# A state-space mixer and a ternary MLP on one core: weight parts and weight copies at other times of a block, and another order in the last step

## The reference, cut to what matters

```python
# layer 1: x + mixer(layernorm(x))
proj = xn @ W_in * mup_vector                      # 512 -> 1024 z, 1280 xBC, 64 dt
xBC = silu(causal_conv(xBC, conv_w, 4 taps) + conv_b)
dt = softplus(dt + dt_bias); dA = exp(dt * -exp(A_log))
state = state * dA_t + (dt_t * x_t) B_t;  y_t = state . C_t      # scan over tokens
g = (y + D * x) * silu(z)
g = g * rsqrt(mean(g * g) + 1e-5) * norm_w
x1 = x + g @ W_out
# layer 2: x1 + mlp(layernorm(x1)), weights of -1, 0 and 1, scales per row
hdn = silu((x1n @ gate_w.T) * gate_s) * ((x1n @ up_w.T) * up_s)
out = x1 + (hdn @ down_w.T) * down_s
```

## Time and profile before

| | us |
|---|---|
| median of 3 runs | 797.53 |
| lowest and highest | 793.96, 797.57 |
| the profiled execution, its own time | 789.45 |
| span of its trace | 787.6 |

### The profile page before, as it was taken

How to read it: one execution, slowest core, us unless ns; L and a number is a source line. 1 busy time by engine, 2 the same in 40 slices (tenths; PEclk the granted TensorE clock), 3 DMA queues, 4 the chain that set the end, 5 groups by cost and what they waited for, 6 DMA issues and landing times.

```text
span 787.6 us, 20256 instructions
## 1 busy us (share of the span) xinstructions
PE 745.6 (95%) x8464; PEld 612.6 (78%) x8464; DVE 521.9 (66%) x843; ACT 493.8 (63%) x941; POOL 292.4 (37%) x232
## 2 busy tenths in 40 slices
PE   5878999999999999999999999689999999999997
PEld 4856878888788888888787887477878878887885
DVE  6878978987977987977988886735423532632331
ACT  6989888877978978978878978623312321321330
POOL 2164186285375465455546636410010011001002
PEclk9988999999999999999999999789999999999999
DMA  9832337637548448348446454685013013003002
GB/s 300 228 85 84 77 93 213 141 87 235 109 96 245 118 95 247 92 100 216 130 115 170 136 117 120 204 276 179 0 55 108 0 42 119 0 13 94 1 1 82
DMA packets 41929, 94.94 MB, mean 121 GB/s; under 512 B 9648, under 2 KB 15280, under 8 KB 41648
## 3 DMA queue, kind: packets, MB, share of 16 engines
q1 hardware_dynamic: 41840, 93.67, 42.6%
HBM read 84.73 MB, written 17.57 MB: 130 GB/s over the span
## 4 chain that ended last, share of the span: by engine, by line
PE 51%; DVE 26%; ACT 8%; DMA 8%; issue 5%; SPq 1%; POOL 0%; DVEq 0%; POOLq 0%; ACTq 0%
DVE cx L874 10%; PE ps_x L1549 10%; PE ps_y L1562 10%; PE ps_proj L1549 8%; PE ps_x L1198 3%; DVE ring L929 3%; PE ps_proj L1149 3%; DVE dt_p L849 3%; PE ps_y L1221 3%; PE ps_proj L1150 3%; PE ps_proj L1151 2%; ACT ring L658 2%; DVE state L939 2%; PE ps_x L1232 2%; ACT sz L601 2%
## 5 line engine op out<-in xcount | busy, mean ns | idle before, releaser
L487 POOL TENSOR_TENSOR ring<-tokd,ring 128x1024 f32<-128x1024 f32 x64 | 123.2, 1937 | 197.0 <-ACT tokd L653 125.8
L1149 PE MATMUL ps_proj<-xn_hi,win_hi 128*128 128x256 f32 x608 | 178.9, 294 | 1.5 <-DVE xn_lo L843 1.5
L1150 PE MATMUL ps_proj<-xn_lo,win_hi 128*128 128x256 f32 x608 | 172.6, 284 | 0.0
L1151 PE MATMUL ps_proj<-xn_hi,win_lo 128*128 128x256 f32 x608 | 172.1, 283 | 0.0
L1149 PEld LDWEIGHTS ps_proj<-xn_hi,win_hi 128*128 128x128 f32 x608 | 116.4, 191 | 15.6 <-issue 11.4
L1150 PEld LDWEIGHTS ps_proj<-xn_lo,win_hi 128*128 128x128 f32 x608 | 116.6, 192 | 0.4
L1151 PEld LDWEIGHTS ps_proj<-xn_hi,win_lo 128*128 128x128 f32 x608 | 116.5, 192 | 0.0
L874 DVE SCALAR_TENSOR_TENSOR cx<-cin,consts,cx 128x256 f32<-128x256 f32 x240 | 96.4, 481 | 0.0
L1440 POOL TENSOR_TENSOR res<-res,hidden 128x512 f32<-128x512 f32 x16 | 20.5, 1283 | 184.0 <-DVE hidden L1503 184.0
L929 DVE TENSOR_TENSOR ring<-ring,ps_tok 128x1024 f32<-128x1024 f32 x64 | 75.6, 1214 | 4.2 <-ACT ring L662 4.2
L658 ACT ACTIVATE ring<-ring 128x1024 f32<-128x1024 f32 x64 | 66.8, 1059 | 10.6 <-POOL ring L487 10.6
(11 more groups left out here) (154 smaller groups left out, 1615.8 us busy)
## 6 DMA issues: line engine op xcount, KB each, us to landing
ring<-cum_dram SPq DMA_DIRECT2D x128, 256.0 KB, 5.4
xin<-x SPq DMA_DIRECT2D x8, 512.0 KB, 4.3
res<-x SPq DMA_DIRECT2D x32, 128.0 KB, 3.0
x_dram<-res SPq DMA_DIRECT2D x32, 128.0 KB, 2.4
x_in_sb<-x_dram SPq DMA_DIRECT2D x4, 1024.0 KB, 5.7
res<-x_dram SPq DMA_DIRECT2D x16, 256.0 KB, 2.7
out<-res SPq DMA_DIRECT2D x16, 256.0 KB, 2.0
gate_w_copy<-gate_w SPq DMA_DIRECT2D x2, 1408.0 KB, 9.1
```

The costliest lines, as they stand in the source:

```text
L487: pool.tensor_tensor(ring[:, g, :, :], own, ring[:, g, :, :], ALU.subtract).then_inc(diffed, 1)
L1149: pe.matmul(out, win_hi[:, k, cols], xn_hi[:, k, :], start=(k == 0), stop=False)
L1150: pe.matmul(out, win_hi[:, k, cols], xn_lo[:, k, :], start=False, stop=False)
L1151: made = pe.matmul(out, win_lo[:, k, cols], xn_hi[:, k, :], start=False, stop=(k == KT - 1))
```

## The change

**Parts.** The 18 parts get widths 1024, 1024 and 768 for each half of a weight, where there were five of 1024 and one of 512. There are still three in a block. Their tiles are now `xin`, `rows` and a tile of their own, `low_buf`. In block i, SP loads the first into `xin` and the third into `low_buf` where it loaded x and the third part before, and the second into `rows` at the end of its list. DVE reduces them a block later: two right after `gate_lo` of the block's start, the third after the first step's gate.

**x and copies.** The x of the next block is loaded at the start of a block, after the first reduction has freed `xin`. The copies are 12 pieces of 704 KB, two at the start of each of the blocks 2 to 7, ahead of the x1 store and the ring loads of step 1.

**Last step.** The gated y of step 15 is split into a part of h_hi and h_lo instead of g_hi and g_lo, and projected into ps_x instead of ps_out, so its split waits neither for `project_out(14)` nor its projection for `make_x1(14)`. The first half of `project_out(14)` stands between carry and add_carry. DVE makes x1 of step 13 before `mix(15, 0)`. The four normalisations of the MLP's input are parted around `gate_lo`, and `any_low` and `make_x1(14)` come later. SP loads x1 for the statistics before it waits for `all_low_max`.

```diff
-LOW_W = 1024
-LOW_EACH = -(-HID * INTER // (P * LOW_W))
+LOW_WIDTHS = (1024, 1024, 768)
+LOW_EACH = 2 * len(LOW_WIDTHS)
 LOW_PARTS = 3 * LOW_EACH
+LOOKED = range(1, 1 + LOW_PARTS // len(LOW_WIDTHS))
+COPIES = 12
...
+        def g_of(c):
+            if c < LAST:
+                return g_hi, g_lo
+            return [t[:, ZT:ZT + 2, :].rearrange("p m (k t) -> p (m k) t", t=P) for t in (hand.h_hi, hand.h_lo)]
+        def out_of(c):
+            return ps_out[:] if c < LAST else ps_x[:, 0:BT]
...
-                w, rows_of = n // 2, slice((n % 2) * (P // 2), (n % 2 + 1) * (P // 2))
+                w, rows_of = n // 4, slice((n % 4) * (P // 4), (n % 4 + 1) * (P // 4))
...
             def body(i, first, last):
-                looking = not first and not last
+                if i - 1 in LOOKED:
+                    if i + 1 < BLOCKS:
+                        sp.wait_ge(hand.low_max_made, 3 * (i - 2) + 1)
+                        load_x(i + 1)
+                    keep_weights(2 * (i - 2))
+                    keep_weights(2 * (i - 2) + 1)
                 if not first:
                     store_x1(i - 1, 0)
                     load_res(i, 0, first)
                 for g in range(GROUPS):
-                    if looking and g == 2:
-                        load_low_rows(3 * (i - 1), STEPS * i)
-                    if looking and g == GROUPS - 1:
-                        load_low_xin(3 * (i - 1) + 1, i)
                     load_cums(i, 1, g)
-                if looking:
-                    keep_weights(i - 1)
...
-                if i + 2 < BLOCKS:
-                    if looking:
-                        sp.wait_ge(hand.low_max_made, 3 * (i - 1) + 2)
+                if i in LOOKED:
+                    load_low_xin(i)
+                    load_low_buf(i)
+                else:
                     load_x(i + 2)
-                if looking:
-                    load_low_rows(3 * (i - 1) + 2, STEPS * i + 1)
...
                 load_whole(i + 1, False)
+                if i in LOOKED:
+                    load_low_rows(i)
...
             body(BLOCKS - 1, False, True)
-            sp.wait_ge(hand.low_all_made, 1)
-            sp.dma_start(hand.low_row[:], hand.low_all[:]).then_inc(hand.low_in, 16)
             sp.wait_ge(projected, EVENTS * BLOCKS)
             sp.dma_start(hand.xin[:], hand.x1_by_block[0]).then_inc(hand.x_in, 16)
...
             load_weights(1)
+            sp.wait_ge(hand.low_all_made, 1)
+            sp.dma_start(hand.low_row[:], hand.low_all[:]).then_inc(hand.low_in, 16)
...
             def gate_hi(c):
                 act.wait_ge(gate_made, c + 1)
-                act.wait_ge(out_made, c)
+                if c < LAST:
+                    act.wait_ge(out_made, c)
...
                 if tiles[0] == 0:
                     pe.wait_ge(g_split, c + 1)
-                    pe.wait_ge(x1_made, c)
+                    if c < LAST:
+                        pe.wait_ge(x1_made, c)
...
                 carry(i, 1)
+                if last:
+                    project_out(c - 1, FIRST_HALF)
...
                     sum_squares(c - 1)
-                    project_out(c - 1)
+                    project_out(c - 1, SECOND_HALF)
```

94 lines of the change are left out of this document (53 added, 41 removed).

## The result

The changed kernel takes 786.97 us, the median of 6 runs (783.21 to 789.96), and the kernel before 795.75 us (792.48 to 798.62, 6 runs) beside it. The ratio is 0.9889 with a 95% interval of 0.9848 to 0.9929: 8.8 us less, and the interval lies wholly under 1. The forecast was 790.4, the range 785.5 to 796.5. Of the 3.4 us between forecast and result about half is in the gain, 8.8 us for 7.1. The other half is in the kernel before, whose median of six is 795.75 where the forecast started from 797.53.

A forecast was written before the change was run, and what follows sets the result against it. PE bounds the kernel, busy for 745.6 of 787.6 us, so only its holes and slow clock can be won. 2.2 us in the blocks plus 4.9 in the last step make 7.1: 797.53 - 7.1 = 790.4 us, range 785.5 to 796.5.

The forecast's parts named there:

- The start of a block: DVE's extra part of 1.21 us at a block's start costs nothing; data up to 0.8 us later cost nothing either.
- the prediction's sign of being wrong: Wrong if PE still waits on DVE at mixer's end, weight loads begin after 506, or rows' part ends DVE idle time.
- slower* rival: At a block's start the part in rows lands late and DVE stalls before xpad: 801.8 us, chance 0.08.
- The middle of a block: Blocks' nine PE holes of 4.3 us shrink as the chain gains 0.3 to 0.4 us a block: 2.2 us, bounds 0 to 4.3.
- The copies: Copies at a block's start, in a window of free DMA, cost nothing, or up to 1 us a block if transfers are slower.
- The first hole: Last step, PE's wait of 2.36 us before carry: stays, and carry stays slow, ending at 500.05.
- The hole at rows: Last step, PE's 3.37 us wait for rows: gone or below 0.5 us, filled by the half projection; rows done at 502.6.
- PE ready for the MLP: Last step, end of PE's chain: ready at about 519.5, 9 us before 528.50.
- The weights: Late next: loads begin at some 503.3, all in at 521.7, MLP at 522.2, 523.6 in effect; gain 4.9 us.
- The second x load: The MLP's second x load comes behind the weights and moves with them.
- second rival: Queue gives it back: x1(13) store waits for 2.7 MB, loads begin at 506.6, 2.8 us gained, 794.7 us; chance 0.2.
- its second term: Last step, up to the MLP's first product: gain 528.5 - 523.6 = 4.9 us, bounds 9 and 2.

The follow-up runs named there:

- copies_mid_fixed: Changed kernel with the two weight copies of blocks 2 to 6 behind the ring loads, those of block 7 still at its start: 787.87 us, 0.9878 to the kernel before.
- blocks_only: Kernel before with the parts, the x load and the copies moved, last step as before: 793.59 us, ratio 0.9951.
- before_again: The kernel before, unchanged, run and profiled once more: 795.51 us.
- tail_only: Kernel before with the last step's edits alone: 792.69 us, ratio 0.9941.
- copies_back: Changed kernel with the two copies of each block behind the ring loads: 791.58 us, 0.9921 to the kernel before.
- after_again: The changed kernel once more, on the same chip as the runs of its two halves: 787.09 us, 0.9879 to the kernel before.
- no_xin_part: Kernel before without the weight part in xin: its load gone, its scan cut to two columns of rows: 792.41 us, ratio 0.9918.
- weights_first: Changed kernel with gate and up weights loaded ahead of the store of x1 of step 13 and the load of res: 788.76 us, 0.9899 to the kernel before.
- half_old: Changed kernel with the whole projection of step 14 behind the groups again: 787.81 us, 0.9877 to the kernel before.
- x1_old: Changed kernel with make_x1(13) behind the first mix, the statistics and the carry's scaling again: 788.86 us, 0.9902 to the kernel before.
- stores_early: Changed kernel with gate and up weights first, and the stores of steps 14 and 15 moved among the down weights: 784.76 us, 0.9827 to the kernel before.
- g_old: Changed kernel with step 15's gated y and projection in the other steps' buffers again, make_x1(14) ahead of the MLP's low halves: 786.08 us, 0.9839 to the kernel before.

## Why the prediction was right, point by point

**The start of a block** is free, as forecast. There is no wait for the part in `rows` but 0.3 us once (up to 1.1 us in the other profiles with these blocks, in copies_mid_fixed), and what DVE waits there for ACT's copy of tok shrank from 17.3 to 8.5 us in the stretch. Taken literally the prediction's sign of being wrong, that this part ends an idle time of DVE, did appear; but up to 0.8 us of it was reckoned as free. The *slower* rival had no part in it.

**The middle of a block** is the term of the sum that was mis-sized: 2.2 us forecast, 3.9 us measured by blocks_only, and 4.0 us by the profiles (369.4 us is the mean of three with the old blocks, before, before_again and tail_only, and 365.4 us that of ten with the new). The step taken, "hardly any of it counts, because gate_lo also waits for ACT's g_hi", is right for g_lo itself: in before g_lo begins 0.03 us after g_hi's end in five of the six blocks. What the sum left out stands behind g_lo. The three dt_p instructions took 1.05 to 2.66 us there for 0.93, 5.0 us too much over the six blocks, next to a last ring that came late behind the load of the part in `xin`. The prediction saw that the rings would come earlier without that load, but put it down as 0.35 us for ScalarE alone. It also read one block. Block 6, which it read, has no hole; block 5 has PE's largest one:

```profile
376.88 2.66 DVE L849 SCALAR_TENSOR_TENSOR dt_p<-dt_p,dt_e 128x128 f32<-128x128 f32 x3
```

```profile
380.93 1.94 PE L1198 MATMUL ps_x<-state,cx 128*64 128x512 f32 x8 [1.45 <-DVE xpad L915]
```

Its upper bound of 4.3 us was the sum of the holes in that execution; 6.6 and 7.0 stood in the next two. The two profiles that the prediction was about show no gain in the blocks at all, 366.34 and 366.38 us.

**The copies** cost nothing in the blocks, as forecast (copies_mid_fixed). That their place in block 7 sets when the weights may be read was not seen; copies_back put 3.3 to 4.5 us on it.

**The first hole** stayed, 2.36 us. The slow carry behind it, 3.38 us before, is 1.94 in the profile of after and 3.46 in after_again; see the last section.

**The hole at rows** was to be gone, or below 0.5 us, and is 1.06 us. The steps were nearly exact. All times in this and the next two points are less 2.70 us, by which after is late at carry 14. DVE has rows done at 502.7 (forecast 502.6). PE has the half projection done at 501.6 where 503.0 was forecast, since the carry ran at full clock; so the 1.06 us are the other side of what the clock saved. In after_again, where the carry took 3.46 us, there is no hole at rows.

**PE ready for the MLP**: 519.5 forecast, 520.7 measured. Two idle times put down to issue, 0.90 and 2.29 us, are in it, and the forecast had neither: its 0.9 us at the last group are for the products themselves. Before had such an idle time as well, 1.50 us inside the groups. What it is stays open.

**The weights** are what is late next, as forecast. Their loads began at 505.2, not at 503.3: the store took 5.55 us behind the 2.7 MB for 3.42 in before, and here the trace agrees with the order of a ring that the prediction drew from the Trainium skill, page "DMA: Bandwidth & Descriptors", section "Queues, rings and completion order". It was the second rival's mechanism, with 1.9 of its 3.3 us. All parts were in at 522.6 (forecast 521.7), since the loads themselves took 17.4 us in place of 18.4, and the MLP began at 523.5 where 522.2 was forecast. The 1.4 us for a slow clock behind that wait did not come (the first eight products take 2.1 us). The two errors cancel: 523.6 in effect against 523.5, and 4.97 us of the gain against 4.9 forecast. tail_only confirms the term by time, 4.7 us.

**The second x load** was said to move with the weights. In after it came 58.95 us after carry 14 (537.00 less 478.05), and in before 62.84 (538.19 less 475.35). So it moved 3.9 of the 5.0 us, and the rest shows as PE's wait of 1.29 us for 0.36. From the row of before:

```profile
538.19 0.39 SPq L1393 DMA_DIRECT2D x_in_sb<-x_dram  x1
```

**Not in the prediction at all**: the stretch up to carry 2, where the change edits no instruction that has run by then, took 111.67 us for 109.01. Over the profiles it is 110.9 us in the mean for the ten kernels with the changed blocks and 109.5 for the other four.

In stages, by means over the profiles, the gain is 4.0 us in the blocks and 5.1 us behind carry 14 (314.5 us in before, before_again, blocks_only and no_xin_part, 309.4 in after, after_again, tail_only and copies_mid_fixed), less 1.4 us at the start: 7.7 us. The forecast of 7.1 us was right for its second term. For the sum it was lucky: 1.8 us too little in the blocks and 1.4 us that it didn't have at the start offset each other. Its chances of faster, 0.57, 0.15 and 0.02, add up to 0.74, not 0.73; nothing hangs on it.

## What to carry to other kernels

One profile is one draw of the transfers' landing times. Where an engine's list waits for a transfer that is only just in time, look at the same wait in every block, not at one that happens to be covered. And follow the engine's list from there to where the bottleneck waits, with the length of every instruction beside its shortest: here the wait in plain sight came to less, in the sums, than three small instructions behind it that had grown from 0.93 to as much as 2.66 us. When a wait at the end of a stage is for transfers, list what stands behind them in the same queue before moving them ahead: the 3.2 us that weights_first won came back at the next thing in that queue.

## What the runs showed of the hardware

**The clock behind one and the same hole fell in some executions and not in others.** In all 14 profiles PE is idle for 2.36 or 2.37 us before the carry of step 15. The carry then takes 1.94 us in six (after, half_old, x1_old, copies_mid_fixed, stores_early, blocks_only) and 2.54 to 3.55 us in the other eight. Granted clock by windows (us; busy PE, PEld, DVE, ACT, POOL; clock, DMA share, GB/s), in after and in before_again:

```profile
496.00:500.00 4.00, 1.64 (x16) 1.10 (x14) 3.81 (x8) 3.97 (x5) 3.63 (x4) 1.00 0.90 291
```

```profile
500.00:504.00 4.00, 3.53 (x8) 0.68 (x8) 2.50 (x4) 4.00 (x5) 3.84 (x4) 0.58 1.04 417
```

The first stays at the level of 2.4 GHz, the second falls towards 1.2. The same kernel had both: 1.94 us in after, 3.46 in after_again. In eight profiles the half projection follows the carry at once, and the two together can be measured, from the carry's start to the end of the twelfth matmul. They take 4.88 to 4.91 us in three (after, copies_mid_fixed, stores_early) and 6.43 to 6.54 us in the other five, with nothing between. Even copies_back, where the carry took only 2.54 us, is one of the five: there the slow clock came later and reached into the half projection. So the price of this hole was nothing or some 1.6 us, and the 1.44 us that the prediction put on every hole of over 2 us is that second value, less what falls behind the carry. What decides between the two, no run here shows.

**VectorE sometimes takes over twice as long for the same instructions.** DVE in before and in after, at the same place in block 0:

```profile
60.16 1.40 DVE L821 SCALAR_TENSOR_TENSOR wout_lo<-skip,consts,wout_hi 128x512 fp32r<-128x512 f32 x2
```

```profile
60.95 3.05 DVE L842 SCALAR_TENSOR_TENSOR wout_lo<-skip,consts,wout_hi 128x512 fp32r<-128x512 f32 x2
```

GpSimd's row at that time, in before and in after:

```profile
60.91 2.41 POOL L487 TENSOR_TENSOR ring<-tokd,ring 128x1024 f32<-128x1024 f32 x1 [2.35 <-DMA ring<-cum_dram]
```

```profile
61.37 2.08 POOL L507 TENSOR_TENSOR ring<-tokd,ring 128x1024 f32<-128x1024 f32 x1 [3.08 <-DMA ring<-cum_dram]
```

Two such instructions take 1.40 us alone. In before both had begun when GpSimd did; GpSimd then took 2.41 us. In after GpSimd began at 61.37, before the second would have, and ended at 63.45; the pair ended at 64.00, as if the second had waited for it. All 14 profiles agree with that: the pair takes over 3 us in the four where GpSimd began ahead of the second instruction (an estimate: half of 1.40 us after the first), and 1.40 us in the ten where it began later. The Trainium skill, page "SBUF — State Buffer", section "Who interferes with whom", says that VectorE with two inputs in SBUF contends with a GpSimd instruction that reads SBUF, and that whoever issues first blocks the other. These rows agree with it; no run here separates it from another cause.

The three dt_p in the middle of a block behave alike. Of the 84 such blocks in the 14 profiles, they take 0.93 to 0.96 us in all 61 where GpSimd's last ring product had ended, or had at most 0.17 us to go, when they began. In the 23 where it had 0.26 us or more to go they take 1.05 to 3.49 us. All 18 blocks of before, before_again and tail_only are among the 23.

Back to the start of the span. The pair takes 3.04 to 3.09 us in after, after_again, stores_early and g_old, but 1.40 us in weights_first and copies_mid_fixed, which are just as late at carry 2. So why the start of six of the ten kernels with the changed blocks is 1 to 3 us longer than in the others stays open.
